# A two-layer graph kernel on one core: one-hots of the second pass a turn ahead, four groups gathered early, cells 11 nodes wide

## The reference

```python
edge_input = jnp.concatenate([x[src], edge_attr], axis=-1)
messages = _gelu(edge_input @ mW1 + mb1) @ mW2 + mb2
gates = jax.nn.sigmoid(_gelu(edge_input @ gW1 + gb1) @ gW2 + gb2)
aggregated = jax.ops.segment_sum(messages * gates, dst, num_segments=x.shape[0])
...
x = _layernorm(x + _L0_gnn_ref(...), axis=-1)
...
norm = dinv[row] * ew * dinv[col]
h = x @ W
out = jax.ops.segment_sum(h[row] * norm[:, None], col, num_segments=N)
...
x = _layernorm(x + out + b, axis=-1)
```

## Time and profile before

| | before |
|---|---|
| median of 3 runs | 1641.46 us (1636.66 to 1643.33) |
| profiled execution: time, span | 1641.43 us, 1639.6 us |
| mean granted TensorE clock | 0.96 of full speed |
| pass 1, last gather issued | 985.03 us |
| pass 2, first and last gather issued | 1030.04 us, 1605.56 us |

### The profile page before, as it was taken

The page is one execution under the profiler, slowest core; times in us unless marked ns, Lnnn a source line. Parts: engine busy times, 40 slices in busy tenths (PEclk is TensorE's granted clock), DMA queues, the critical chain, the costliest instruction groups (busy, mean ns, idle before and its releaser), DMA issues.

```text
span 1639.6 us, 31556 instructions
## 1 busy us (share of the span) xinstructions
PE 1435.3 (88%) x11180; PEld 1273.6 (78%) x11181; DVE 1143.4 (70%) x3201; ACT 559.8 (34%) x985; POOL 1178.4 (72%) x1257
## 2 busy tenths in 40 slices
PE   3526999999999999999999987899999999998996
PEld 2415878787878778787877776799998989887986
DVE  5314889888988888889888887444654556555543
ACT  1103545454544545454544443111111111212110
POOL 7777777777777777777777770677777777777771
PEclk8767999999999999999999999999999999999997
DMA  3423444344444444444444443454544435353530
GB/s 106 123 67 109 133 120 131 115 134 116 134 117 126 124 127 125 115 134 118 133 116 127 122 116 115 130 173 125 168 143 126 165 104 167 101 191 102 196 112 19
DMA packets 80039, 205.95 MB, mean 126 GB/s; under 512 B 39325, under 2 KB 40893, under 8 KB 76703
## 3 DMA queue, kind: packets, MB, share of 16 engines
q1 hardware_dynamic: 28688, 127.68, 20.5%
q0 software_dynamic: 39808, 61.22, 17.4%
q10 hardware_dynamic: 11376, 14.90, 3.1%
HBM read 139.91 MB, written 63.80 MB: 124 GB/s over the span
## 4 chain that ended last, share of the span: by engine, by line
DVE 37%; PE 34%; DVEq 14%; issue 7%; DMA 3%; another core or an unknown queue 2%; POOL 2%; ACT 1%; ACTq 0%; POOLq 0%
DVE shared L1137 8%; PE ps_bt L642 8%; PE ps_win L730 5%; PE ps_xt L645 5%; PE ps_hid L645 4%; DVE logit L1126 4%; DVE shared L1133 3%; DVE edges L1102 3%; DVEq L1125 3%; PE ps_hid L625 3%; PE ps_xt L625 3%; DVEq L1049 2%; DVE prod L1123 2%; DVEq L1100 2%
## 5 line engine op out<-in xcount | busy, mean ns | idle before, releaser
L430 POOL DMA_INDIRECT rows<-in_x_nat,idx x782 | 740.5, 947 | 243.0 <-issue 237.0
L430 POOL DMA_INDIRECT rows<-x1s_table,idx x462 | 436.0, 944 | 184.6 <-issue 139.9
L546 PE MATMUL ps_hid<-w,edges 128*128 128x192 f32 x1568 | 325.2, 331 | 0.0
L546 PEld LDWEIGHTS ps_hid<-w,edges 128*128 128x128 f32 x1568 | 272.2, 194 | 14.3 <-issue 1.3
L1137 DVE TENSOR_TENSOR shared<-cell,ps_fix 128x1200 f32<-128x1200 f32 (+1 forms) x128 | 218.3, 1706 | 0.0
L784 ACT ACTIVATE edges<-ps_hid 128x768 f32<-128x768 f32 x196 | 159.1, 812 | 172.1 <-PE ps_hid L546 171.1
L1281 DVE TENSOR_TENSOR acc<-acc,ps_win 96x80 f32 x98 | 22.9, 234 | 240.2 <-PE ps_win L721 217.0
L493 PE MATMUL ps_win<-hot,edges 128*98 128x80 f32 x1568 | 156.1, 254 | 28.7 <-DVE acc L1051 28.6
L493 PEld LDWEIGHTS ps_win<-hot,edges 128*98 128x98 f32 x1568 | 148.8, 170 | 40.8 <-DVE edges L1102 39.1
L520 PE MATMUL ps_xt<-ident,rows 128*96 128x128 f32 x784 | 108.9, 284 | 71.9 <-ACT shared L824 40.2
L520 PEld LDWEIGHTS ps_xt<-ident,rows 128*96 128x96 f32 x784 | 89.2, 131 | 87.1 <-ACT shared L824 50.4
(11 more groups left out here) (157 smaller groups left out, 2241.8 us busy)
## 6 DMA issues: line engine op xcount, KB each, us to landing
b_table<-shared SPq DMA_DIRECT2D x96, 600.0 KB, 3.4
edges<-b_table SPq DMA_DIRECT2D x12, 2400.0 KB
wide<-b_table SPq DMA_DIRECT2D x12, 2400.0 KB
rows<-in_x_nat,idx POOLq DMA_INDIRECT x782, 2.7
edges<-in_edge_t ACTq DMA_DIRECT2D x96, 128.0 KB
rows<-x1s_table,idx POOLq DMA_INDIRECT x462
wide<-in_x_t SPq DMA_DIRECT2D x1, 2376.5 KB
out_nodes<-y SPq DMA_DIRECT2D x49, 48.0 KB
```

The costliest lines, as they stand in the source:

```text
L430: nc.gpsimd.indirect_dma_start(out=rows[slot][:, k, :], out_offset=None, in_=table, in_offset=bass.IndirectOffsetOnAxis(ap=idx[:, TG * g + ...
L546: mm = nc.tensor.matmul(ps_hid[j][:, HC * q:HC * (q + 1)], feat[u][:, P * m:P * (m + 1)], w1[:, :], start=False, stop=(q == 1))
```

## The change

`WD` goes from 12 to 11, which narrows every B matrix: a half of a tile's cells from 300 to 275 columns, B in the sums from 96 to 88, and `b_table` by a twelfth.

One built group, group 44 (place 18 in the list of dense ones), is no longer dense: 39 dense turns, 15 of them built, 24 stored as before. The gathered groups are 59 instead of 58. Four of them, groups 1, 4, 6 and 7 (`EARLY`), are gathered **early**, after pass 1's last gather and before `x1s_table` is complete, from a second table `x1s_early`. SP writes the first 43 blocks (`DONE_B`) of it during pass 1, and a row of zeros behind them; a source in a later block points to that row. What the last 6 blocks add to these four groups is made like a small built group (`early_hots`, `early_cells`, `early_sums`, `early_placed`), two groups at the end of turn 1 and two at the end of turn 3. 

The one-hots of gathered groups are made a turn ahead, in four buffers instead of two, and how many groups each turn takes is a list (`TAKES`). In a turn before a built one, DVE makes the gathered one-hots and the end of the norm after the turn's additions. The two `If`s are one (`run`). The last turn is a dense one, whose two gathered groups stand behind its sums; two parts of the output (3 and 2 blocks) are left for after it, where it was one part of 3.

```diff
-WD = 12
+WD = 11
...
-FIRST_BUILT = KINDS.index("B")
-NONE_YET = (0, 1)
-ONE_MORE = (12, 22, 32)
 MIXED = NG // ROW * ROW
-DENSE = [g for g in range(MIXED) if g % ROW in STARTS]
-KIND = [KINDS[d % len(KINDS)] for d in range(len(DENSE))]
+SITES = [g for g in range(MIXED) if g % ROW in STARTS]
+LEFT_OUT = (18,)
+SITE = [i for i in range(len(SITES)) if i not in LEFT_OUT]
+DENSE = [SITES[i] for i in SITE]
+KIND = [KINDS[i % len(KINDS)] for i in SITE]
 NTURN = len(DENSE)
 BUILT = [d for d in range(NTURN) if KIND[d] == "B"]
 STORED = [d for d in range(NTURN) if KIND[d] == "P"]
-GATHERED = [g for g in range(NG) if g not in DENSE]
-DT = NTURN * TG
+FIRST_BUILT = BUILT[0]
+EARLY = (1, 4, 6, 7)
+NE = len(EARLY)
+DONE_B = 43
+LATE_B = NB - DONE_B
+LATE_C = LATE_B * WD
+GATHERED = list(EARLY) + [g for g in range(NG) if g not in DENSE and g not in EARLY]
+DT0 = len(SITES) * TG
+DT = DT0 + NE * TG
 PAIRS = len(STORED) * TG // 2
 PAIR_AT = 2
 CELLS = 2 * HW
...
+EARLY_IN = {BUILT[0]: (0, 1), BUILT[1]: (2, 3)}
+TAKES = (0, 0, 2, 2, 1, 2, 1, 1, 1, 2, 2, 2, 2, 2, 0, 2, 1, 1, 2, 2, 2, 2, 2, 2, 2, 1, 0, 2, 2, 2, 1, 0, 2, 1, 2, 2, 2, 2, 2)
+HOTS = 4
...
+            step1(0, 0, True, None)
+            eng.wait_ge(s_steer, 1)
...
+                for g in range(1, NG):
+                    step1(g // SLOTS, g % SLOTS, True, beside(g))
+                end1()
+                usual2()
...
+            sp.wait_ge(s_zero, 1)
+            sp.dma_start(x1s_early[DONE_B * P:(DONE_B + 1) * P, :], y[:, 0, :]).then_inc(s_zeroed, 16)
...
+                    b = n // 2 - LAG - 1
+                    if n % 2 == 0 and 0 <= b < DONE_B:
+                        sp.wait_ge(s_xs, b + 1)
+                        sp.dma_start(x1s_early[P * b:P * (b + 1), :], x_nat[:, b, :]).then_inc(s_early, 16)
...
+            def early_gathers(i):
+                for k in range(TG):
+                    nc.gpsimd.indirect_dma_start(
+                        out=rows[slot_of(i)][:, k, :], out_offset=None, in_=x1s_early,
+                        in_offset=bass.IndirectOffsetOnAxis(ap=idx_early[:, TG * i + k:TG * i + k + 1], axis=0)).then_inc(
+                            s_rows2[i % SLOTS], 16)
...
+                pool.wait_ge(s_zeroed, 16)
+                pool.wait_ge(s_early, 16 * DONE_B)
+                for i in range(NE):
+                    pool.wait_ge(s_xt, NG - SLOTS + i + 1)
+                    early_gathers(i)
+                pool.wait_ge(s_xt, NG)
                 pool.wait_ge(s_xsw, 16 * NB)
                 for i, g in enumerate(GATHERED):
                     if i >= SLOTS:
                         pool.wait_ge(s_acc2, PLACE[GATHERED[i - SLOTS]] + 1)
-                    gathers(g, i % SLOTS, x1s_table, s_rows2)
+                    if i >= NE:
+                        gathers(g, slot_of(i), x1s_table, s_rows2, i % SLOTS)
...
+            def early_cells(e):
+                wait(pe, s_early_out, e - 1)
+                for k in range(TG):
+                    if k % (TG // 2) == 0:
+                        pe.wait_ge(s_early_hot, 2 * e + 2 * k // TG + 1)
+                    c = LATE_C * (k % (TG // 2))
+                    mm = nc.tensor.matmul(ps_pair[e % 2][:, k // (TG // 2), c:c + LATE_C], hot_low[:, k, :], early_place[:, k, :],
+                                          start=True, stop=True)
+                    if k % (TG // 2) == TG // 2 - 1:
+                        mm.then_inc(s_early_cells, 1)
+
+            def early_sums(q, es, e):
+                pe.wait_ge(s_early_out, e + 1)
+                if e == es[0]:
+                    pe.wait_ge(s_rowsumc, q + 1)
+                for c in range(LATE_B):
+                    mm = nc.tensor.matmul(ps_bt[0:TW, ND * e:ND * (e + 1)], early_b[e % 2][:, TW * c:TW * (c + 1)],
+                                          x_nat[:, DONE_B + c, :], start=(c == 0), stop=(c == LATE_B - 1))
+                mm.then_inc(s_early_sums, 1)
+
+            def early_placed(q, es):
+                pe.wait_ge(s_early_rows, early_part_of[es[0]] + 1)
+                pe.wait_ge(s_early_node, 1)
+                for m, e in enumerate(es):
+                    col = len(TURNS2[q]) + m
+                    nc.tensor.matmul(ps_win[0:ND, W * col:W * (col + 1)], early_rows[:, e, :], early_node[:, e, :],
+                                     start=True, stop=True)
+
+            def early_part(q, es):
+                for e in es:
+                    early_cells(e)
+                for e in es:
+                    early_sums(q, es, e)
+                early_placed(q, es)
...
-                    if q == NTURN:
-                        turn_over(q - 1)
-                        place_sums(q - 1)
-                        outputs(q - 1)
-                        gathered_of(turn)
-                    elif KIND[q] == "B":
+                    if KIND[q] == "B":
                         dense_cells(q)
                         gathered_of(turn)
                         dense_sums(q, range(0, NB))
+                        if q in EARLY_IN:
+                            early_part(q, EARLY_IN[q])
...
-                        gathered_of(turn)
+                        if q < NTURN - 1:
+                            gathered_of(turn)
                         outputs(q - 1)
                         dense_sums(q, range(SUMS_AFTER, NB))
-                outputs(NTURN)
-            run_pass(pe, step2, block2, usual=usual2)
+                        if q == NTURN - 1:
+                            gathered_of(turn)
+                turn_over(NTURN - 1)
+                place_sums(NTURN - 1)
+                outputs(NTURN - 1)
...
+            def early_hots(e, m):
+                ks = range(TG // 2 * m, TG // 2 * (m + 1))
+                first = [es[0] for es in EARLY_IN.values()]
+                if e in first:
+                    dve.wait_ge(s_cells, TG * first.index(e) + TG // 2 * (m + 1))
+                else:
+                    dve.wait_ge(s_early_cells, 2 * (e - 1) + m + 1)
+                t0 = DT0 + TG * e
+                for k in ks:
+                    nc.vector.tensor_scalar(hot_low[:, k, :], places_ps[:, 0:P], src_low[:, t0 + k:t0 + k + 1],
+                                            weight[:, TG * EARLY[e] + k:TG * EARLY[e] + k + 1], ALU.is_equal, ALU.mult)
+                shape = [P, TG // 2, LATE_C]
+                nc.vector.tensor_tensor(early_place[:, ks[0]:ks[-1] + 1, :], cell[:, t0 + ks[0]:t0 + ks[-1] + 1, 1:2].to_broadcast(shape),
+                                        places_ps[:, 0:LATE_C].rearrange("p (o w) -> p o w", o=1).to_broadcast(shape),
+                                        ALU.is_equal).then_inc(s_early_hot, 1)
...
+            def gathered_of(q):
+                if q < NTURN:
+                    for g in TURNS2[q]:
+                        if g not in DENSE:
+                            gathered2(GATHERED.index(g), g)
...
+                    makes = q > 0 and q + 1 < NTURN and KIND[q + 1] == "B"
+                    if q == 0:
                         node2(q)
-                    for g in turn:
-                        if g not in DENSE:
-                            gathered2(GATHERED.index(g), g)
-                    if q + 1 < NTURN and KIND[q + 1] == "B" and q + 1 != FIRST_BUILT:
+                        dense2(FIRST_BUILT, 1)
+                        for e in EARLY_IN[FIRST_BUILT]:
+                            for m in range(2):
+                                early_hots(e, m)
+                    elif makes:
                         for m in range(2):
                             dense2(q + 1, m)
-                    for b, n, ready, _ in PARTS:
-                        if ready == q - 1:
-                            block2(list(range(b, b + n)))
+                    else:
+                        if q == FIRST_BUILT:
+                            early_nodes()
+                        gathered_of(q + 1)
+                        if q in EARLY_IN and q != FIRST_BUILT:
+                            for e in EARLY_IN[q]:
+                                for m in range(2):
+                                    early_hots(e, m)
+                    if q > 0:
+                        node2(q)
+                    parts = [list(range(b, b + n)) for b, n, ready, _ in PARTS if ready == q - 1]
+                    for part in parts:
+                        block2_sum(part)
+                        if not makes or part is not parts[-1]:
+                            block2_norm(part)
                     nodes = [first_node(g) for g in turn]
+                    if q in EARLY_IN:
+                        early_first = [first_node(EARLY[e]) for e in EARLY_IN[q]]
+                        dve.wait_ge(s_win3, PLACE[turn[-1]] + 1)
+                        for m, node in enumerate(early_first):
+                            col = len(turn) + m
+                            nc.vector.drain()
+                            nc.vector.tensor_tensor(acc1[0:ND, ds(node, W)], acc1[0:ND, ds(node, W)],
```

(7 more changed lines are left out.)

198 lines of the change are left out of this document (126 added, 72 removed).

## The result

| | before | after |
|---|---|---|
| median of the comparison | 1642.38 us (7 runs) | 1630.20 us (1628.72 to 1634.19, 7 runs) |
| ratio to before | 1 | 0.9931, 95% interval 0.9914 to 0.9947 |
| span of the profiled execution | 1639.6 us | 1630.4 us |
| pass 1, last gather issued | 985.03 us | 985.00 us |
| first and last gather from `x1s_table` | 1030.04, 1605.56 us | 1029.40, 1585.34 us |

The change makes the kernel 0.7% faster. Forecast was 1610 us, range 1599 to 1629. The direction came, but only 12 of the 31 us.

The account below looks back on a forecast made before the run. PE, its waits included, was taken to bind pass 2, POOL next. PE's terms took 1616.9 to 1583 us; POOL's slot wait put the products' end at 1589; adding 18.8 and 1.8 gave 1610 us, range 1599 to 1629.

Parts of the forecast that it names:

- the bullet on one-hots: Pass 2, PE: one-hots made a turn ahead remove waits and slow records, -23 us; DVE has time enough.
- A wait for rows or for a 2.2 MB load of B in a short P turn ... adds 1.5: Pass 2, PE: waiting for gathered rows or a stored B's load adds 1.5 us in all.
- late norms: Pass 2, sign of being wrong: DVE's norms come late and PE waits for them in each built turn.
- Stored sums: Pass 2, PE: sums with a loaded B, 88 moving columns for 96, keep their pace of 85 ns: 0 us.
- Built sums: Pass 2, PE: sums with a built B, 88 stationary columns for 96, go at 82 ns a record: -5 us.
- Cells at 0.98 us a tile: Pass 2, PE: cells of 275 columns for 300 take 0.98 for 1.04 us a tile, 116 tiles: -7 us.
- Early parts of 8.5 us: Pass 2, PE, turns 1 and 3: two added parts of about 8.5 us each, +17 us.
- The joined `If`: Start of pass 2: DVE's one-hots start 1.9 us earlier, PE's first cells with them or more: -3 us.
- the slot wait: Pass 2, POOL near 1090 us: the seventh new-table group waits 7.3 us for an early group's slot, not regained.
- Rival 4: Early gathers do not run in the gap; POOL has 59 groups from 1030 on: 1642 us, no change, chance 0.04.
- The tail: From the end of the last gathered products to the end of the span, with a second output part: 18.8 us.
- rival 5: Pass 2: waits leave PE at the lower clock level for 600 records, 46 us more: 1656 us, chance 0.08.

Follow-up runs that it names:

- The first experiment: The changed kernel with SP issuing a turn's output stores one turn later, behind the next load of B: 1613.82 us, ratio 0.9837.
- the run with four held loads: The changed kernel with only its list of turns changed from turn 13 on, so stores hold back four B loads instead of eight: 1626.47 us, ratio 0.9901.

## Why the prediction was wrong

**The step that failed** is in the bullet on one-hots: "DVE is busy 299 of 550 us, so it holds". I asked whether DVE's deferred work would be late for PE, and put it at nothing. I did not ask who else waits for it. The end of the norm releases SP's stores, and behind them in the same queue the load of a B. The term "A wait for rows or for a 2.2 MB load of B in a short P turn ... adds 1.5" measured 23.0 us, with about 9 us of slow records behind it. Among what could prove me wrong I named late norms, but with PE waiting for them "in each B turn", not for the load behind them. The first experiment shows the step alone: without the hold the changed kernel takes 1613.8 us, within 4 of the forecast. Part of that nearness is luck: its gathered products end at 1595.8 us, 7 later than the 1589 of the sum, and its tail is 0.5 shorter. What is left is at least in part the rows, 8.8 us of waits there, which the same term of 1.5 us was to cover: I had PE and POOL ending at 1583 and 1586, and yet counted hardly any waits between them.

**PE's other terms.** No waits for one-hots: right. Stored sums unchanged at 85 ns: right. Built sums, here at turn 17: 8.26 us for 98 records against the 8.51 of the earlier trace rows, 2.6 ns a record less where I took 3 (82 ns): right at 15 x 0.25 = 3.8 us for 5. The Trainium skill, "TensorE: Matmul & The Clock Gate", section "LDWEIGHTS (loading the stationary operand)", has columns / 1.2, 73 ns for loading 88 columns; the pace of the sums did not fall to that, but to 82 or 83 ns. That their 96 moving columns hold it there, as the forecast took, fits, but no run changes these alone. Cells at 0.98 us a tile: right. Early parts of 8.5 us: the first took from 1045.14 to 1053.51, 8.4, the second from 1083.70 to 1093.71, 10.0, with part of its sums at the lower clock. Their effect on the time, 11 us, was in the sum as 17. The joined `If`: the first cells of pass 2 stand at 1031.9 for 1036.0 before, 4 us for 3.

**POOL's side** was right but for one step: 32 gathers from 986.25 on, 1029.4, the slot wait (8.4 for 7.3), and the end; the second slot wait, 2.7 us, was not in it. Rival 4 was right as a price (1643.3 against 1642) and did not happen. **The tail** was 17.6 for 18.8. **Pass 1** did not move.

**The width**, -7 and -5 us in the sum and "0" for the stored sums, is worth 4 us alone; in the kernel before, waits for rows take 3.0 of the rest, as I had said of POOL ("next with little room") without using it for parts of the change.

**The clock**, rival 5: the mechanism is there behind six of the eight waits, but with 0.98 in the stretch it cost 9 us, not 46. The kernel before has it too: four stretches of records 160 ns apart between 1250 and 1600 us, behind waits for one-hots, some 7 us together. Those 6 us of the forecast's 23 did go, and came back behind the loads.

## What to carry over

When work is deferred on an engine with time to spare, list everything that its result releases, and everything queued in order behind those waiters: here a norm some 6 us later cost 12 us of time, through a store ahead of a load in one DMA queue. Put loads that feed the bounding engine ahead of stores that nobody waits for. And a table that sets turns moves more than the work it names; work out from it which waits it creates, before trusting a plan that looks at one of them.

## What was unexpected in the hardware

Six of PE's eight waits of 1.6 to 3.7 us for a late load are followed by records at the lower of the two clock levels (22 in 2.90 us against 2.03), which adds some 40% to the 23 us of waits, and the granted clock of a long stretch, 0.98, hides it. And one chip ran each of four kernels 1.53 to 1.57 times slower: with PE idle for 2.48 us between single products, no semaphore outstanding, at a granted clock of 0.50, while POOL kept its 1.25 us per gather. On it the variants of the changed kernel were 34 us slower than the kernel before; in the run with four held loads all of that stood there already when pass 2 began (the first load of a B at 1517.7 us, against 1480.7 in the kernel before with its loads first). Why, stays open.
